# K's copies moved from ScalarE to VectorE, Gelu's table and first call moved up, the norms' last step written as two tensor_tensor operations

## The reference

```
# layer 0: residual block of three convolutions with batch norm
h = relu(bn(conv1x1(x)));  h = relu(bn(conv3x3_grouped(h)));  x = relu(bn(conv1x1(h)) + x)
# layer 1: shifted 7x7 window attention (8 heads of 16) and an MLP (128 -> 512 -> 128)
y   = layernorm(x) rolled by (-3, -3), cut into windows of 49 tokens
q, k, v = y @ qkv_w.T
p   = softmax(q k^T * 16**-0.5 + relative bias + mask)
x   = x + unroll((p v) @ proj_w.T + proj_b)
out = x + gelu(layernorm(x) @ fc1_w.T + fc1_b) @ fc2_w.T + fc2_b
```

## Time and profile before

| | |
|---|---|
| median of 3 runs | 5091.67 us (5086.66 to 5092.45) |
| profiled execution, time / span | 5094.79 us / 5093.0 us |
| PE busy | 4619.0 us, 91% of the span |
| DVE busy | 3638.2 us, 71% |
| ACT busy | 3552.5 us, 70% |
| POOL busy | 2603.1 us, 51% |
| TensorE clock granted, mean | 0.98 |

### The profile page before, as it was taken

How to read it: one execution, slowest core, us unless ns; L and a number is a source line. 1 busy time by engine, 2 the same in 40 slices (tenths; PEclk the granted TensorE clock), 3 DMA queues, 4 the chain that set the end, 5 groups by cost and what they waited for, 6 DMA issues and landing times.

```text
span 5093.0 us, 197119 instructions
## 1 busy us (share of the span) xinstructions
PE 4619.0 (91%) x73232; PEld 3246.6 (64%) x73232; DVE 3638.2 (71%) x7458; ACT 3552.5 (70%) x5899; POOL 2603.1 (51%) x3504
## 2 busy tenths in 40 slices
PE   2788888599999999999999999999999999999998
PEld 1555655466666666666666666666666666666665
DVE  2233333378888888888888888888888888888886
ACT  0333333377777777777777777777777777777776
POOL 5233333255555555555555555555555555555554
PEclk7899999799999999999999999999999999999999
DMA  2334443100000000000000000000000000000000
GB/s 65 104 123 133 129 132 126 54 24 27 27 27 27 27 27 27 27 27 27 27 27 27 27 27 27 27 27 27 27 27 27 27 27 27 27 27 27 27 27 23
DMA packets 304839, 219.23 MB, mean 43 GB/s; under 512 B 49306, under 2 KB 252010, under 8 KB 304682
## 3 DMA queue, kind: packets, MB, share of 16 engines
q1 hardware_dynamic: 304682, 216.79, 14.4%
HBM read 111.12 MB, written 111.94 MB: 44 GB/s over the span
## 4 chain that ended last, share of the span: by engine, by line
PE 59%; DVE 20%; issue 11%; ACT 5%; SPq 2%; DVEq 1%; POOL 1%; DMA 0%; ACTq 0%; POOLq 0%
DVE xn L1063 8%; PE bank L602 8%; PE bank L683 7%; PE bank L658 6%; PE bank L535 5%; PE bank L594 4%; DVE sc L1038 4%; PE bank L625 4%; PE bank L548 4%; PE bank L674 4%; PE bank L585 3%; PE bank L612 3%; DVE z L1063 3%; ACT L851 2%; PE bank L637 2%
## 5 line engine op out<-in xcount | busy, mean ns | idle before, releaser
L1063 DVE SCALAR_TENSOR_TENSOR xn<-x,lnp 98x128 f32<-98x128 f32 x1024 | 873.5, 912 | 3.7 <-POOL lnp L1133 3.7
L1202 POOL TENSOR_TENSOR res<-x,projb 98x512 f32<-98x512 f32 x256 | 325.9, 1273 | 1014.5 <-DVE x L1080 1014.5
L1220 POOL TENSOR_TENSOR sc<-sc,mx 128x784 f32<-128x784 f32 x512 | 788.6, 1541 | 54.7 <-DVE mx L1044 54.7
L683 PE MATMUL bank<-g,fc_sb 128*128 128x392 f32 x2048 | 784.6, 506 | 0.1
L1038 DVE TENSOR_TENSOR sc<-bank,shared 128x392 f32<-128x392 f32 x1024 | 530.0, 560 | 310.6 <-PE bank L612 310.5
L851 ACT ACTIVATE g<-bank,fc1b 128x392 f32<-128x392 f32 x1024 | 574.7, 586 | 124.6 <-PE bank L676 111.1
L674 PE MATMUL bank<-zt_hi,fc_hi 128*128 128x392 f32 x1024 | 452.1, 441 | 153.8 <-ACT g L851 148.5
L625 PE MATMUL bank<-ident_sb,sc 128*113 128x128 f32 x4096 | 530.9, 273 | 0.3 <-ACT shared L861 0.3
L1133 POOL TENSOR_TENSOR lnp<-st 98x8 f32<-98x8 f32 x777 | 146.2, 217 | 746.8 <-DVE st L916 746.8
L625 PEld LDWEIGHTS bank<-ident_sb,sc 128*113 128x113 f32 x4096 | 515.3, 177 | 2.5 <-ACT shared L861 0.7
L1044 DVE TENSOR_REDUCE mx<-sc 128x16 f32<-128x784 f32 x512 | 496.6, 970 | 18.4
(11 more groups left out here) (103 smaller groups left out, 9185.9 us busy)
## 6 DMA issues: line engine op xcount, KB each, us to landing
x<-x_scratch SPq DMA_DIRECT2D x768, 49.0 KB
out_x<-y SPq DMA_DIRECT2D x672, 49.0 KB
xc_even<-in_x SPq DMA_DIRECT2D x128, 196.0 KB
shared<-in_x SPq DMA_DIRECT2D x128, 196.0 KB
x_scratch<-xc_even SPq DMA_DIRECT2D x128, 196.0 KB
x_scratch<-shared SPq DMA_DIRECT2D x128, 196.0 KB
x<-x_scratch SPq DMA_DIRECT2D x256, 38.5 KB
out_x<-y SPq DMA_DIRECT2D x224, 38.5 KB
```

The costliest lines, as they stand in the source:

```text
L683: mm = nc.tensor.matmul(RC[:, 0:ST], fc2[:, c, :], g[:, c], start=c == 0, stop=c == HC - 1)
L1063: ins = V.scalar_tensor_tensor(dst[:, p, :], src[:, p, :], lnp[:, 7, i, p:p + 1], lnp[:, 8, i, p:p + 1].to_broadcast([PT, C]), ALU.add, AL ...
L1220: P.tensor_tensor(out=s_r, in0=s_r, in1=m_r.to_broadcast([128, 2 * HEADS, N]), op=ALU.subtract).then_inc(sub_done, 1)
```

## The change

On ACT, Gelu's table is asked for by name right behind the high part of z, and Gelu of part 0 comes next; its half of V follows, and then Gelu of parts 1 and 2. K is no longer ACT's: DVE makes the same two masked copies, with tensor_scalar, in front of its half of V. The norms' last step is two tensor_tensor operations over all four pairs (98x512): the broadcast negm is added, a semaphore is waited for, and the result is multiplied in place by the broadcast rstd. In the program after, x2_norm and x1_norm name a semaphore each for this step. PE's, POOL's and SP's orders are unchanged.

```diff
--- before.py
+++ after.py
@@ -261,6 +261,7 @@
         wrapped = sem("wrapped")
         stats = [sem(f"stats_sem{i}") for i in range(2)]
         small = sem("small")
+        xn_centred, z_centred = sem("xn_centred"), sem("z_centred")
         xn_sb, z_sb, res1_sb, res2_sb = sem("xn_sb"), sem("z_sb"), sem("res1_sb"), sem("res2_sb")
         a_full, a_out, c_full, c_out = sem("a_full"), sem("a_out"), sem("c_full"), sem("c_out")
         hidden_full, hidden_out = sem("hidden_full"), sem("hidden_out")
@@ -833,13 +834,6 @@
                 nc.scalar.activation(vb[QROWS:VT, t.u, :, :, 1], RB[0][QROWS:VT, :].rearrange(
                     "p (w q d) -> p w q d", w=WINS, q=QUADS), ACT.Copy).then_inc(b_out[0], 1)
 
-            def k_out(t):
-                act.wait_ge(a_full, A_JOBS * t.n + 3)
-                for hh in range(2):
-                    i = nc.scalar.activation(km[:, :, hh, :], RA[:, 0:ST].rearrange("c (w n) -> c w n", n=N),
-                                             ACT.Identity, scale=headmask[:, hh:hh + 1])
-                i.then_inc(a_out, 1)
-
             def zt_out(t):
                 act.wait_ge(c_full, C_JOBS * t.n + 1)
                 nc.scalar.activation(zt_hi[:], RC[:, 0:ST], ACT.Copy).then_inc(c_out, 1)
@@ -880,11 +874,12 @@
                     q_out(t)
                 if t3.there():
                     zt_out(t3)
-                if t.there():
-                    k_out(t)
+                    nc.scalar.preload_act_table_set("gelu_and_others")
+                if t3.there():
+                    gelu(t3, 0)
+                if t.there():
                     v_out(t)
                 if t3.there():
-                    gelu(t3, 0)
                     gelu(t3, 1)
                     gelu(t3, 2)
                 if t1.there():
@@ -1013,6 +1008,13 @@
                 i.then_inc(biasm_done, 1)
                 dve.wait_ge(biasm_done, 1)
 
+            def k_out(t):
+                dve.wait_ge(a_full, A_JOBS * t.n + 3)
+                for hh in range(2):
+                    i = V.tensor_scalar(km[:, :, hh, :], RA[:, 0:ST].rearrange("c (w n) -> c w n", n=N),
+                                        headmask[:, hh:hh + 1], None, ALU.mult)
+                i.then_inc(a_out, 1)
+
             def v_out(t):
                 dve.wait_ge(b_full[0], 4 * t.n - 2 if t.c or not t.fixed else 1)
 
@@ -1056,21 +1058,21 @@
                 wait(dve, small, SMALL * t.n)
                 norm_stats(0, t, x1[:, t.u])
 
-            def norm(i, round_, src, dst, done):
+            def norm(i, n, round_, src, dst, centred, done):
 
                 dve.wait_ge(small, SMALL * round_ + SMALL)
-                for p in range(PAIRS):
-                    ins = V.scalar_tensor_tensor(dst[:, p, :], src[:, p, :], lnp[:, 7, i, p:p + 1],
-                                                 lnp[:, 8, i, p:p + 1].to_broadcast([PT, C]), ALU.add, ALU.mult)
-                ins.then_inc(done, 1)
+                negm, rstd = [lnp[:, k, i].unsqueeze(2).to_broadcast([PT, PAIRS, C]) for k in (7, 8)]
+                V.tensor_tensor(out=dst[:], in0=src, in1=negm, op=ALU.add).then_inc(centred, 1)
+                dve.wait_ge(centred, n + 1)
+                V.tensor_tensor(out=dst[:], in0=dst[:], in1=rstd, op=ALU.mult).then_inc(done, 1)
 
             def x1_norm(t):
                 wait(dve, a_full, A_JOBS * (t.n - 1) + 1)
-                norm(0, t.n, x1[:, t.u], xn, xn_sb)
+                norm(0, t.n, t.n, x1[:, t.u], xn, xn_centred, xn_sb)
 
             def x2_norm(t):
                 wait(dve, c_full, C_JOBS * (t.n - 1) + 1)
-                norm(1, t.n + 3, x2, z, z_sb)
+                norm(1, t.n, t.n + 3, x2[:], z, z_centred, z_sb)
 
             def x2_out(t):
                 dve.wait_ge(b_full[1], 4 * t.n + PROJECTION + 1)
@@ -1095,6 +1097,7 @@
                 if t3.there():
                     zt_rest(t3)
                 if t.there():
+                    k_out(t)
                     v_out(t)
                 if ahead.there():
                     x1_stats(ahead)
```

## The result

The changed kernel takes 5394.92 us (median of 4 runs, 5392.67 to 5402.02), the kernel before 5092.06 us beside it. The ratio is 1.060, with a 95% interval of 1.0581 to 1.0618: slower by 303 us. The forecast was 5361 us, with 5240 to 5450 as its range, and 0.91 for slower.

The account below looks back on a forecast made before the run. A turn was the larger of PE's own work (15.15 us) and DVE's loop (11.59 + N). N of 5.33 gave 16.92, 1.06 more; 254 turns gave +269, so 5364, less 3 for the median: 5361 us, range 5240 to 5450.

Parts of the forecast that it names:

- a turn: From one output projection's start to the next: 15.86 us on average before, 16.92 forecast, over some 254 turns.
- DVE's loop: PE from projection through scores, then DVE's bias, maxima, xn, z and ot, to the next projection: 11.59 us plus N.
- PE's own work: PE's work in a turn without its waits for Gelu and ot: 15.15 us, the least a turn can be.
- N: Time from xn's first instruction to ot's start on DVE: 4.38 us before, forecast 5.33.
- Its price when free: One tensor_tensor of the norms' last step on DVE, not held by POOL: 0.69 us.
- its 0.55 us after a release: A held tensor_tensor on DVE ends 0.15 + 0.40 = 0.55 us after the POOL operation that held it.
- Rival 1: The norms' tensor_tensor on DVE is not held by POOL: N 2.70 us, 4911 us in all; chance 0.06.
- POOL's lateness: V and statistics stand behind K on DVE, so POOL's factors and first subtract start 0.44 us later.
- rival 2: Xn's add slips between POOL's operations, or POOL is less late or not lengthened: 5250 to 5330 us; chance 0.25.
- The sign that I had named: Mark of a right forecast in the profile after: turns of 16.9 us, all alike.
- rival 4: Early Gelu still gains its 0.58 us a turn beside the longer norms: about 5215 us; chance 0.05.
- the forecast's own case: Xn's add held through both subtracts, its multiply by residual2: 5361 us, range 5330 to 5400; chance 0.5.

Follow-up runs that it names:

- runs 4 (second): Kernel before with only ACT's half of V moved behind Gelu 0, K first and the table load behind it: 5089.64 us, ratio 1.0000.
- 6: Kernel before with POOL's residual2 moved from behind the subtracts to the head of POOL's turn: 5014.26 us, ratio 0.9849.
- 7: Residual2 first in POOL: kernel before, V behind Gelu 0, 4893.88 us; K on DVE, early Gelu, old norms, statistics first, 4876.22; changed kernel 5057.45, with statistics first 4994.02.
- run 1: Kernel before with only the norms' last step as two tensor_tensor: 5230.11 us, ratio 1.0274.
- run 5 with one matmul: Changed kernel with one throwaway 128x512 matmul on constants in front of PE's output projection: 5325.29 us, ratio 1.0458 to the kernel before.
- Run 2: Changed kernel with the norms' last step back to four scalar_tensor_tensor: 5171.35 us, ratio 1.0155 to the kernel before.

## Why the prediction was right, and where it was off

**What bounds the kernel.** That a turn is the larger of DVE's loop and PE's own work held throughout; runs 4 (second), 6 and 7 show it from both sides. One reading was wrong: I took the shorter kind of turn (15.74) for PE's own with one wait in it. It was DVE's loop too, only 0.23 us shorter, and removing PE's wait did nothing to it. So the 11.59 us of DVE's loop outside N hold for the longer kind alone; in the shorter kind they are 15.74 - 4.38 = 11.36.

**The norms' new form.** Its price when free, 0.69 us, its 0.55 us after a release and the 0.40 us by which it lengthens POOL's operation were all measured as worked out (0.68 and 0.69; 0.54 and 0.55; 1.72 and 1.73 for 1.32). Rival 1, in which it isn't held, is refuted by run 1 and by the rows after.

**K on DVE and where the engines meet.** K was expected to end in time, or to slip by 0.05 us; it slips by 0.09. POOL's lateness came as forecast: its first factor starts 0.38 us later behind the scores' end (0.4 was the forecast). But I had walked through one turn only, one of the longer kind, and taken all turns for alike. What I described for it, xn's add held through both subtracts, came true in the other kind. In the longer kind the add slipped in between the subtracts, which is rival 2, and two things that I left out met there. DVE reaches xn later in the turns whose bias it picks by a register, by 0.23 us before and 0.34 after (why it is 0.11 more now is open). And an add that is issued with so little of subtract 0 left gets in before subtract 1. The sign that I had named, all turns alike, holds for their length (16.76 and 16.77) and not for what happens in them.

**The early Gelu.** That it buys nothing beside the longer loop is shown for the kernel before by the second run 4. For rival 4, in which it gains beside the longer norms, nothing speaks: DVE's loop in the change adds up without it (11.45 + 5.31 and 11.79 + 4.99).

**The sum.** The turns gave +230 us where I had 269. N is 5.15 us on average for 5.33, 46 us less over 254 turns. The rest of DVE's loop is 11.62 on average for 11.59, and that it came so near is luck: 11.59 was 0.115 too much for the mean of both kinds, and K's 0.09 and the 0.11 in every second turn made up for it. The term that I didn't have is the clock: PE's wait for ot was in the forecast, at 1.8 us a turn, but not what it does to PE, 75 us, which I had priced at nothing. The two errors go opposite ways, and the median lies 34 us above the forecast. Without the clock it would have been about 5320 us, which is where run 5 with one matmul stands (5325). That is in the range of rival 2, below the 5330 to 5400 of the forecast's own case. So the direction and the price of a hold were foreseen; that the time fell within the own case is luck.

The Trainium skill, "TensorE: Matmul & The Clock Gate", section "What's actually happening", has the half rate as the state without activity, and activity as what ends it. The trace agrees on the two levels (0.50 and 1.00). Here it needed no long gap: the longest of PE's waits between 1500 and 4500 us was 1.7 us.

## What to carry to other kernels

When a VectorE operation with two SBUF inputs takes far longer than its sisters, look at what GpSimd does just then. Here fewer, longer operations made it worse (140 us), and a change in GpSimd's order gave more than any change of the operation did. A wait that is removed from an engine pays only if that engine's loop is the longest; here the same edit was worth 0 and then 120 us. A new wait on TensorE may not be free even where it is covered (75 us here): look at the granted clock. And when turns come in two kinds, walk through one of each before you forecast.

## What of the hardware I had not expected

Whether DVE gets in between POOL's two back-to-back subtracts went with how late it asked. Over all turns of the change in which xn's first operation was issued during subtract 0, it was held through both subtracts in the 127 where 0.34 us or more of subtract 0 was left (0.36 in the turn above, 11.41 against its end at 10.25 + 1.52 = 11.77), and got in between in the 126 where 0.30 us or less was left (28.50 against 28.69). Run 2 has 129 and 126 cases, with the border between 0.31 and 0.32 us.

That the time left is the cause is not shown. xn is issued some 0.08 us before the end of the maxima that release subtract 1, in every one of these turns, so how early subtract 1 was ready has the same border (it was ready early where DVE was held), and no run here tells the two apart. The two groups are also the two kinds of turn, but for one turn in each group of the change and one in run 2. And the border doesn't hold for the next pair: between subtract 1 and residual2 the held instruction got in each time in the turns shown, in the second turn with 1.35 us of subtract 1 left when it was issued (29.26 against 27.17 + 3.44 = 30.61).

The Trainium skill, "SBUF — State Buffer", section "Who interferes with whom", has the shared port locked for the whole of one instruction. The trace agrees that one blocks the other fully; but here one operation was held through two, which that rule alone doesn't give.
